# From step 12 on, the causal mask is copied into the scores' bank instead of multiplied in, and the queries' rotation stands earlier in half of the steps

## The chip, the cores and the metric

The kernel runs on one core of a Trainium2 chip. The metric is the device time of one execution in microseconds. The kernel before takes 309.91 us (median of 3 runs, 309.84 to 309.98). Five engines work side by side, each through its own queue in a fixed order: TensorE (PE: matrix products and turns; its weight loads are listed as PEld), VectorE (DVE), ScalarE (ACT), GpSimd (POOL) and SyncE (SP, which issues the DMAs). They wait for each other by counters (semaphores).

## The reference

A block of a decoder layer on x (16 sequences of 64 tokens, 256 wide) with a context of 64 tokens per sequence: gated attention, then a gated feed-forward.

```python
def attention(x, ctx, wq, wk, wv, wo, wk_ctx, wv_ctx, q_norm_w, k_norm_w):
    q = rms_norm(x @ wq, per head of 128, q_norm_w)              # 16 heads
    k = rms_norm(x @ wk, per head of 128, k_norm_w)              # 4 key heads
    v = x @ wv
    k_ctx = rms_norm(ctx @ wk_ctx, per head, k_norm_w); v_ctx = ctx @ wv_ctx
    q = q * cos + rotate_half(q) * sin                           # also k, not k_ctx
    scores = q @ concat(k_ctx, k) * scale + mask                 # 64 x 128 keys for a sequence and head
    # mask: 0 for the context's keys, causal (-inf above the diagonal) for the own keys
    return softmax(scores) @ concat(v_ctx, v) @ wo

x = x + tanh(g_xattn) * attention(layernorm(x), ctx, ...)
gate = silu((h @ fp8(gate_w)) * gate_scale); up = (h @ fp8(up_w)) * up_scale   # h = layernorm(x)
x = x + tanh(g_ffn) * ((gate * up) @ fp8(down_w)) * down_scale
```

## The kernel before

**Tiles and steps.** The 1024 tokens are 8 tiles of 128 (two sequences each). A tile takes four steps, one for each key head and the four query heads that use it. Steps are numbered k = 0 to 31; m = k // 4 is the tile and j = k % 4 the place in it, so "j 0" is a tile's first step and "j 3" its last. In the same four steps the keys and values of the next tile are made and the feed-forward of the tile before is worked off in pieces. Each engine's queue is the same function `one_step` written out for every k, and the order of lines in it is the order of its queue: nothing is scheduled by a program.

**One step on PE.** (1) It turns `q_rot`, the rotated queries of this step (L432), (2) projects the queries of the next step into bank `ps_q` (L409, L414), (3) applies the output projection to the attention of the step before (`ot_hi` by L453, the low part `ot_lo` by L462), (4) turns what is due in this place (`xn` in j 0 and j 2, `k_sin`, the own keys, in j 3), (5) makes the scores in bank `ps_s`, (6) turns the probabilities `probs` of the step before, (7) takes a piece of the feed-forward (`ps_ff`, L561; in j 1 and j 2 behind the next part), (8) projects a part of keys or values and (9) multiplies the turned probabilities `pt` by the values (L752).

**The scores' bank.** `ps_s` holds 128 rows (two sequences of 64 queries) by four heads of 128 keys. Two bf16 matmuls put the mask where own keys stand (L699); they open the bank, and 16 f32 matmuls of keys and queries (L704) add on top. These 18 use tiles of 64 columns of PE's array (in the rows of the profile: 128\*64), everything else on PE uses 128\*128.

**The softmax's loop over the engines.** DVE takes the rows' maximum from `ps_s` (L1245) and makes `exp_bias` (L1248). ACT takes the exponential in four parts (`probs`, L950). DVE inverts the sums (`row_inv`, L1304), POOL multiplies them in (L1470). In the next step PE turns `probs`, and ACT copies them out as `pt` (L926).

**The queries' way.** PE's projection into `ps_q` releases `q_made`. ACT squares it and sums (L785, four ACTIVATEs with their sums; `q_squared`), DVE multiplies `ps_q` by cosine and sine (`q_rot` L1105, `q_sin` L1109), POOL adds the two (L1426), and PE turns the sum as the first thing of the next step. Before the change DVE waits for `q_squared`, so the rotation is behind ACT's squares. From the sum of squares DVE makes `ssq_eps` (L1274) and POOL the scale `q_scale` (L1377), which goes into `exp_bias`.

**Other names that stand around the change.** On DVE: `ot_lo` (L1159); the gate and `fuse` of the feed-forward (L1121 `const`, L1137 `fuse`), whose result the feed-forward on PE waits for one piece later; `xt_lo`<-`ps_transposed` (L1229, j 0), the low part of the tokens turned in this step; `k_var` (L1236, j 2), from which POOL makes `k_inv` for the own keys; `xn` (L1185, j 3), the normalized tokens that PE turns in the next step. On POOL `fuse_lo` (L1388) and `probs` (L1470). On ACT `ot_hi` (L862), `qt` (L869, the copy of the turned queries), `fuse_hi` (L794), and up to step 15 one `o_hi` of 128x1024 a step (L773), while the output weights are still being split.

Of the kernel before, what the change touches and what calls it, by code (L numbers as in the profile page):

```python
# [12 lines left out]
P = 128  # L13
# [81 lines left out]
def build(nc, x, ctx_in, wq, wk, wv, wo, wk_ctx, wv_ctx,  # L95
# [5 lines left out]
    with ExitStack() as stack:  # L101
        def sb(name, shape, dt=f32):
            return stack.enter_context(nc.sbuf_tensor(name, shape, dt))
# [4 lines left out]
        def sem(name):  # L108
            return stack.enter_context(nc.semaphore(name))
# [294 lines left out]
        def _(pe):  # L404
# [225 lines left out]
            def one_step(u, k):  # L630
# [60 lines left out]
                if is_step(u, k):  # L691
# [4 lines left out]
                    scores = four(ps_s)  # L696
                    for r in range(2):
                        rows = slice(r * LEN, (r + 1) * LEN)
                        nc.tensor.matmul(scores[rows, :, rows], ident_bf[:, rows],  # L699
                                         mask[:, :].unsqueeze(1).broadcast_to([P, HPG, LEN]),  # L700
                                         start=True, stop=False, skip_group_check=True)
# [65 lines left out]
        def _(act):  # L767
# [47 lines left out]
            def square_queries(u, k):  # L815
# [3 lines left out]
                if is_step(u, k + 1):  # L819
                    act.wait_ge(q_made, step(u, k + 1) + 1)  # L820
                    if is_step(u, k):
# [25 lines left out]
            def one_step(u, k):  # L847
# [152 lines left out]
        def _(dve):  # L1000
# [95 lines left out]
            def rotate_queries(u, k):  # L1096
# [67 lines left out]
            def one_step(u, k):  # L1164
# [11 lines left out]


                if j == 3 and is_tile(u, m + 2):
                    dve.wait_ge(ln_inv_ready, tile(u, m + 2) + 1)
# [36 lines left out]

                if at_step(u, k) != 0:
                    rotate_queries(u, k)
# [6 lines left out]


                if j == 0 and is_tile(u, m + 1) and tile(u, m + 1) >= TOKENS_SPLIT_FROM:
                    dve.wait_ge(xt_hi_ready, tokens_split(tile(u, m + 1)))
                    nc.vector.tensor_tensor(xt[1][:, nxt, 0:KC, :].rearrange("p c n -> p (c n)"), ps_t[:, 0:HID],  # L1229
                                            as_f32(xt[0][:, nxt, 0:KC, :].rearrange("p c n -> p (c n)")), ALU.subtract)\  # L1230
                        .then_inc(xt_lo_ready, 1)

                if j == 2 and is_tile(u, m + 1):
                    dve.wait_ge(ks_squared, tile(u, m + 1) + 1)
                    dve.wait_ge(kc_inv_ready, tile(u, m + 1) + 1)
                    nc.vector.tensor_scalar(k_var[:, :], k_ssq[:, :], 1.0 / DIM, RMS_EPS, ALU.mult, ALU.add)\  # L1236
                        .then_inc(ks_var_ready, 1)

# [12 lines left out]
                if at_step(u, k) == 0:  # L1251
                    rotate_queries(u, k)


                if j == 2 and is_tile(u, m + 2):
# [119 lines left out]
        def _(pool):  # L1375
# [3 lines left out]
            def fuse_rest(u, slot):  # L1379
# [22 lines left out]
            def one_step(u, k):  # L1402
# [9 lines left out]


                fuse_rest(u, FF_LATE.get(k - 1))

# [7 lines left out]

                if is_step(u, k + 1):
                    pool.wait_ge(q_sin_ready, step(u, k + 1) + 1)
                    nc.gpsimd.tensor_tensor(q_rot[:, :, :], q_rot[:, :, :], q_sin[:, :, :], ALU.add)\  # L1426
                        .then_inc(q_rot_ready, 1)

# [43 lines left out]


            def first_roots():

# [89 lines left out]
```

## Time and profile before

| what | us |
|---|---|
| median of 3 runs | 309.91 (309.84 to 309.98) |
| the profiled execution: its own time | 310.24 |
| its span, first to last instruction | 308.0 |
| around the span | 2.24 |
| PE busy | 294.0 (95%) |
| ACT busy | 232.1 (75%) |
| DVE busy | 231.3 (75%) |
| POOL busy | 183.4 (60%) |
| granted TensorE clock | 1.000 |

The span is one execution as the hardware profiler took it. Busy is the time in which an engine ran an instruction; PE's ends of matmuls are modelled, so where it matters the distance from one start to the next is read instead. A row of the timeline gives start and duration in us and, in brackets, the idle time ahead of it with what ended that. A row of the lines or of a source gives count, busy time and mean. The granted clock is 1.000 throughout, the upper of its two levels (2.4 GHz), so that no part of the time hangs on it.

### The profile page before, as it was taken

To read this page: it belongs to the slowest core of one execution; us is meant where nothing else is said; L and a number is where in the kernel's file an instruction comes from. 1 tells how busy PE (TensorE), PEld (TensorE's weight loads), DVE (VectorE), ACT (ScalarE), POOL (GpSimd) and SP (SyncE) were. 2 spreads that over 40 slices of the span, in tenths; PEclk is the share of its full clock that TensorE was granted. 3 is DMA by queue.
4 is the path that set the end of the run, shared out by engine and by line. 5 is a ranking of instruction groups with operands and counts; after the bars stand their busy time and mean duration, and the time that the engine had idled before them with its cause. 6 is when DMAs were issued, how large, how long until landed. Compare 5 with 4: busy or idle time off the path is not lost.

```text
span 308.0 us, 6587 instructions
## 1 busy us (share of the span) xinstructions
PE 294.0 (95%) x2243; PEld 235.3 (76%) x2243; DVE 231.3 (75%) x482; ACT 232.1 (75%) x893; POOL 183.4 (60%) x178
## 2 busy tenths in 40 slices
PE   7898989998999999999999999999999999988876
PEld 3345666666877888888888888888888888877865
DVE  1768997899899987879864876768765975686553
ACT  2586889977879788998887778787887678776632
POOL 1446685677648695567755685457746684556230
PEclk9999999999999999999999999999999999999999
DMA  6999000000000010001000010000000000000001
GB/s 198 388 390 397 24 17 2 0 1 10 11 3 1 2 34 2 0 2 36 2 0 2 0 37 0 3 0 20 2 1 2 0 19 2 2 0 19 0 0 36
DMA packets 6720, 12.84 MB, mean 42 GB/s; under 512 B 800, under 2 KB 4256, under 8 KB 6688
## 3 DMA queue, kind: packets, MB, share of 16 engines
q1 hardware_dynamic: 6688, 12.43, 11.3%
q8 instruction: 18, 0.29, 0.4%
q14 instruction: 14, 0.11, 0.1%
HBM read 11.38 MB, written 1.05 MB: 40 GB/s over the span
## 4 chain that ended last, share of the span: by engine, by line
PE 28%; ACT 28%; DVE 26%; issue 8%; POOL 5%; DMA 2%; SPq 1%; DVEq 0%; POOLq 0%
ACT probs L950 11%; ACT squares L785 6%; PE ps_y L446 4%; DVE row_max L1245 4%; DVE exp_bias L1248 4%; DVE q_sin L1109 4%; DVE q_rot L1105 3%; ACT qt L869 3%; PE ps_attn L752 3%; PE ps_scores L704 3%; ACT const L842 2%; PE ps_transposed L432 2%; PE ps_kv L420 2%; DMA q_raw<-in_wq_dram 2%; PE ps_probs L432 2%
## 5 line engine op out<-in xcount | busy, mean ns | idle before, releaser
L950 ACT ACTIVATE probs<-ps_scores,exp_bias,q_scale 128x128 f32<-128x128 f32 x128 | 56.9, 455 | 23.7 <-DVE exp_bias L1248 23.6
L1426 POOL TENSOR_TENSOR q_rot<-q_rot,q_sin 128x512 f32<-128x512 f32 x31 | 40.0, 1292 | 18.4 <-DVE q_sin L1109 18.1
L1470 POOL TENSOR_TENSOR probs<-probs,row_inv 128x512 f32<-128x512 f32 x32 | 36.2, 1133 | 17.9 <-DVE row_inv L1304 17.8
L1377 POOL TENSOR_TENSOR q_scale<-ssq_eps,minus_half 128x4 f32<-128x4 f32 x32 | 39.8, 1244 | 10.6 <-DVE ssq_eps L1274 9.6
L1388 POOL TENSOR_TENSOR fuse_lo<-fuse,fuse_hi 128x256 fp32r<-128x256 f32 x21 | 15.4, 733 | 41.3 <-ACT fuse_hi L794 41.3
L785 ACT ACTIVATE squares<-ps_q 128x128 bf16<-128x128 f32 x128 | 34.1, 292 | 5.8 <-PE ps_q L414 4.1
L752 PE MATMUL ps_attn<-pt,values 128*128 128x256 f32 x128 | 33.4, 383 | 0.0
L704 PE MATMUL ps_scores<-kt,qt 128*64 128x128 f32 x512 | 33.3, 273 | 0.0
L926 ACT ACTIVATE pt<-ps_probs 128x512 f32<-128x512 f32 x32 | 19.2, 600 | 13.3 <-PE ps_probs L432 13.3
L704 PEld LDWEIGHTS ps_scores<-kt,qt 128*64 128x64 f32 x512 | 28.9, 137 | 0.0
L1105 DVE TENSOR_TENSOR q_rot<-ps_q,rope 128x512 f32<-128x512 f32 x31 | 21.3, 686 | 9.7 <-ACT squares L785 9.7
L785 ACT ACTIVATION_READ_ACCUMULATOR squares<-ps_q 128x1 f32 x128 | 27.8, 222 | 0.0
L752 PEld LDWEIGHTS ps_attn<-pt,values 128*128 128x128 f32 x128 | 23.1, 190 | 5.4 <-issue 2.9
L950 ACT ACTIVATION_READ_ACCUMULATOR probs<-ps_scores,exp_bias,q_scale 128x1 f32 x128 | 25.7, 201 | 0.0
L1377 POOL TENSOR_TENSOR k_inv<-k_var,minus_half 128x4 f32<-128x4 f32 x16 | 16.6, 1038 | 12.0 <-DVE k_var L1340 5.3
L1304 DVE RECIPROCAL row_inv<-row_sum 128x4 f32<-128x4 f32 x32 | 5.6, 174 | 24.1 <-ACT probs L950 24.1
L1245 DVE TENSOR_REDUCE row_max<-ps_scores 128x4 f32<-128x512 f32 x32 | 21.8, 681 | 1.5 <-PE ps_scores L704 1.5
L453 PE MATMUL ps_y<-o_hi,ot_hi 128*128 128x256 f32 x88 | 22.0, 285 | 0.2 <-ACT ot_hi L862 0.2
L432 PE MATMUL ps_probs<-const,probs 128*128 128x128 f32 x128 | 21.0, 286 | 1.1 <-POOL probs L1470 1.1
L453 PE MATMUL ps_y<-o_lo,ot_hi 128*128 128x256 f32 x88 | 21.4, 278 | 0.0
L409 PE MATMUL ps_q<-q_hi,xt_hi 128*128 128x512 f32 x48 | 21.0, 436 | 0.4 <-issue 0.4
L785 ACT ACTIVATE squares<-ps_kv 128x128 bf16<-128x128 f32 x60 | 15.9, 290 | 7.2 <-DVE k_sin L1206 4.5
(195 smaller groups left out, 839.2 us busy)
## 6 DMA issues: line engine op xcount, KB each, us to landing
q_raw<-in_wq_dram SPq DMA_DIRECT2D x4, 512.0 KB, 8.3
o_raw<-in_wo_dram SPq DMA_DIRECT2D x4, 512.0 KB, 12.3
ctx_t<-in_ctx_dram SPq DMA_DIRECT2D x8, 128.0 KB, 2.7
out_dram<-x_sb SPq DMA_DIRECT2D x8, 128.0 KB, 1.7
stage<-in_gate_w_dram SPq DMA_DIRECT2D x2, 384.0 KB, 10.1
stage<-in_up_w_dram SPq DMA_DIRECT2D x2, 384.0 KB, 11.1
x_sb<-in_x_dram SPq DMA_DIRECT2D x1, 768.0 KB, 13.1
stage<-in_down_w_dram SPq DMA_DIRECT2D x2, 384.0 KB, 13.1
```

The source lines that it names most:

```text
L409: nc.tensor.matmul(dst, lhs(0, i), rhs(b, i), start=(i == 0 and b == 0), stop=False)
L432: last = nc.tensor.matmul(dst[:, i * P:(i + 1) * P], src, ident, start=True, stop=True, is_transpose=True)
L453: nc.tensor.matmul(ps_y[:, 0:HID], ot_hi[:, h, :], w_o[b][:, g0, h, :], start=(g0 == 0 and h == 0 and b == 0), stop=False)
L704: last = nc.tensor.matmul(scores[r * LEN:(r + 1) * LEN, h, :], qt[:, r, h, :], kt[:, par, j, 2 * r:2 * r + 2, :], start=False, stop=(h == ...
L752: last = nc.tensor.matmul(ps_o[:, r * 256:(r + 1) * 256], values[:, p0, r, g0 * DIM:(g0 + 1) * DIM], pt[:, :].rearrange("p (h r l) -> p r ...
L785: last = nc.scalar.activation(squares[:, h, :], src[:, h * DIM:(h + 1) * DIM], ACT.Square, accum_out=dst[:, h:h + 1])
L950: last = nc.scalar.activation(probs[:, i, :], ps_s[:, i * P:(i + 1) * P], ACT.Exp, bias=exp_bias[:, i:i + 1], scale=q_scale[:, k % 2, i:i ...
L1105: nc.vector.tensor_tensor(q_rot[:, :, :], four(ps_q), over_heads(rope[:, 0, :]), ALU.mult)\
L1245: nc.vector.tensor_reduce(row_max[:, :], four(ps_s), AX.X, ALU.max).then_inc(max_ready, 1)
L1377: return nc.gpsimd.tensor_tensor(dst, src, minus_half[:, 0:src.shape[1]], ALU.pow)
L1426: nc.gpsimd.tensor_tensor(q_rot[:, :, :], q_rot[:, :, :], q_sin[:, :, :], ALU.add)\
L1470: nc.gpsimd.tensor_tensor(probs[:, :, :], probs[:, :, :], row_inv[:, :].unsqueeze(2).broadcast_to([P, 4, P]), ALU.mult).then_inc(probs_rea ...
```

## The change

**The mask (k from 12 to 31, 20 steps).** The two mask matmuls are left out. GpSimd fills an f32 tile `mask_all` of 128x128 once, in the prologue (one memset and two small copies; const in SBUF as source). In each of these steps an engine copies it, repeated over four heads, into `ps_s` (128x512): VectorE in j 0, 1 and 3, behind `ot_lo` (15 steps), ScalarE in j 2, behind `qt` (5 steps). The copy waits for `exp_ready` of the step before (the exponential has read the bank), the scores wait for `mask_set` of the copy, and add onto what it wrote.

**The rotation (`ROTATE_FIRST`: k = 12, 15, 16, 19, 20, 23, 24, 27, 28, 31; the last has no next queries).** DVE's `q_rot` and `q_sin` stand directly behind the mask copy, ahead of `xn`, the gate and `fuse`, and wait for `q_made` instead of `q_squared`; POOL's addition stands ahead of `fuse_lo`. ACT's squares in turn wait for `q_sin_ready`. PE's next projection into `ps_q` waits for `q_squared` too, and so does `ssq_eps` (both in all steps).

**Two operations moved in all steps.** DVE's `xt_lo` of the tokens (j 0) and `k_var` (j 2) stand behind `row_max` and `exp_bias` instead of ahead of them.

```diff
+ROTATE_FIRST = tuple(k for k in range(12, STEPS) if k % GROUPS in (3, 0))
+MASK_COPIED_FROM = 12
...
 # PE
                     if is_step(u, k):
                         pe.wait_ge(q_sin_ready, step(u, k) + 1)
+                        pe.wait_ge(q_squared, step(u, k) + 1)
...
-                    for r in range(2):
+                    if step(u, k) >= MASK_COPIED_FROM:
+                        pe.wait_ge(mask_set, step(u, k) - MASK_COPIED_FROM + 1)
+                    for r in range(2 if step(u, k) < MASK_COPIED_FROM else 0):
...
 # ACT: square_queries
                 if is_step(u, k + 1):
-                    act.wait_ge(q_made, step(u, k + 1) + 1)
+                    if step(u, k) in ROTATE_FIRST:
+                        act.wait_ge(q_sin_ready, step(u, k + 1) + 1)
+                    else:
+                        act.wait_ge(q_made, step(u, k + 1) + 1)
...
 # ACT: behind qt
+                if is_step(u, k) and step(u, k) >= MASK_COPIED_FROM and j == 2:
+                    act.wait_ge(exp_ready, step(u, k))
+                    act.wait_ge(mask_filled, 1)
+                    nc.scalar.activation(four(ps_s), mask_all[:, :].unsqueeze(1).broadcast_to([P, HPG, P]), ACT.Copy)\
+                        .then_inc(mask_set, 1)
...
 # DVE
+            def set_mask(s):
+                if s == MASK_COPIED_FROM:
+                    dve.wait_ge(mask_filled, 1)
+                dve.wait_ge(exp_ready, s)
+                nc.vector.tensor_copy(four(ps_s), mask_all[:, :].unsqueeze(1).broadcast_to([P, HPG, P])).then_inc(mask_set, 1)
...
-                    dve.wait_ge(q_squared, step(u, k + 1) + 1)
+                    if step(u, k) in ROTATE_FIRST:
+                        dve.wait_ge(q_made, step(u, k + 1) + 1)
+                    else:
+                        dve.wait_ge(q_squared, step(u, k + 1) + 1)
...
+                if is_step(u, k) and step(u, k) >= MASK_COPIED_FROM and j != 2:
+                    set_mask(step(u, k))
+                if at_step(u, k) in ROTATE_FIRST:
+                    rotate_queries(u, k)
                 if j == 3 and is_tile(u, m + 2):
                     dve.wait_ge(ln_inv_ready, tile(u, m + 2) + 1)
...
                 if is_step(u, k + 1):
                     if is_step(u, k):
                         dve.wait_ge(q_scale_ready, step(u, k) + 1)
+                    dve.wait_ge(q_squared, step(u, k + 1) + 1)
                     nc.vector.tensor_scalar(ssq_eps[:, :], ssq[:, :], DIM * RMS_EPS, None, ALU.add)\
                         .then_inc(ssq_moved, 1)
...
 # POOL
+                if at_step(u, k) in ROTATE_FIRST:
+                    add_rotated(u, k)
                 fuse_rest(u, FF_LATE.get(k - 1))
...
+                if at_step(u, k) not in ROTATE_FIRST:
+                    add_rotated(u, k)
```

DVE's queue in step 12 (j 0), the kernel before; `const` is the gate's product, `ps_ff` a bank of the feed-forward:

```order
193 L1159 TENSOR_TENSOR ot_lo<-ps_attn,ot_hi 128x2x4x64 [waits ot_hi_ready]
194 L1121 SCALAR_TENSOR_TENSOR const<-const,ps_ff 128x256 [waits tanh_ready]
195 L1137 SCALAR_TENSOR_TENSOR fuse<-const,fuse_scale,ps_ff 128x128 [waits fuse_lo_ready,gated_ready]
197 L1105 TENSOR_TENSOR q_rot<-ps_q,rope 128x512 [waits q_turned,q_squared]
198 L1109 TENSOR_TENSOR q_sin<-ps_q,rope 128x512 [waits q_rot_ready]
199 L1229 TENSOR_TENSOR xt_lo<-ps_transposed,xt_hi 128x256 [waits xt_hi_ready]
200 L1245 TENSOR_REDUCE row_max<-ps_scores 128x4 [waits scores_made]
201 L1248 SCALAR_TENSOR_TENSOR exp_bias<-row_max,q_scale 128x4 [waits q_scale_ready,max_ready]
202 L1274 TENSOR_SCALAR ssq_eps<-ssq 128x4 [waits q_scale_ready]
```

The same step of the changed kernel (its line numbers are its own):

```order
193 L1189 TENSOR_TENSOR ot_lo<-ps_attn,ot_hi 128x2x4x64 [waits ot_hi_ready]
194 L1099 COPY ps_scores<-mask_all 128x512 [waits exp_ready,mask_filled]
195 L1135 TENSOR_TENSOR q_rot<-ps_q,rope 128x512 [waits q_turned,q_made]
196 L1139 TENSOR_TENSOR q_sin<-ps_q,rope 128x512 [waits q_rot_ready]
197 L1151 SCALAR_TENSOR_TENSOR const<-const,ps_ff 128x256 [waits tanh_ready]
198 L1167 SCALAR_TENSOR_TENSOR fuse<-const,fuse_scale,ps_ff 128x128 [waits fuse_lo_ready,gated_ready]
200 L1270 TENSOR_REDUCE row_max<-ps_scores 128x4 [waits scores_made]
201 L1273 SCALAR_TENSOR_TENSOR exp_bias<-row_max,q_scale 128x4 [waits q_scale_ready,max_ready]
202 L1282 TENSOR_TENSOR xt_lo<-ps_transposed,xt_hi 128x256 [waits xt_hi_ready]
203 L1312 TENSOR_SCALAR ssq_eps<-ssq 128x4 [waits q_squared,q_scale_ready]
```

Three operations of 128x512 (the copy, `q_rot`, `q_sin`) now stand between `ot_lo` and the gate, none between `fuse` and `row_max`. In j 3 it is the same with `xn` behind `q_sin`.

PE's queue in step 15 (j 3), the kernel before, around the mask:

```order
569 L432 MATMUL ps_transposed<-const,k_sin 128x128 [waits ks_ready,qt_ready]
570 L432 MATMUL ps_transposed<-const,k_sin 128x128 x3
571 L699 MATMUL ps_scores<-mask,ident_bf 64x4x64 x2
572 L704 MATMUL ps_scores<-kt,qt 64x128 x8
573 L432 MATMUL ps_probs<-const,probs 128x128 [waits probs_ready]
```

The same place of the changed kernel (each of the rows of the scores counts pairs, one matmul for each sequence):

```order
565 L439 MATMUL ps_transposed<-const,k_sin 128x128 [waits ks_ready,qt_ready]
566 L439 MATMUL ps_transposed<-const,k_sin 128x128 x3
567 L714 MATMUL ps_scores<-kt,qt 64x128 [waits mask_set]
568 L714 MATMUL ps_scores<-kt,qt 64x128 x7
569 L439 MATMUL ps_probs<-const,probs 128x128 [waits probs_ready]
```

The two mask matmuls are gone and the first of the scores waits for the copy.

## Rows read from the trace of the kernel before

**Rows 1.** The page: busy time of the engines, and the chain that ended last
```profile
PE 294.0 (95%) x2243; PEld 235.3 (76%) x2243; DVE 231.3 (75%) x482; ACT 232.1 (75%) x893; POOL 183.4 (60%) x178
PE 28%; ACT 28%; DVE 26%; issue 8%; POOL 5%; DMA 2%; SPq 1%; DVEq 0%; POOLq 0%
```
**Rows 2.** Windows, tiles 4 and 5: window, length, busy, PEclk
```profile
157.30:192.14 34.84, 34.69 (x290) 30.06 (x289) 24.57 (x55) 27.49 (x113) 21.65 (x23) 1.00 0.03 9
192.14:226.60 34.46, 34.46 (x289) 30.06 (x288) 24.57 (x55) 27.11 (x112) 21.54 (x22) 1.00 0.02 6
```
**Rows 3.** Timeline of PE around the mask, step 23: start, us, engine, line
```profile
221.26 0.60 PE L432 MATMUL ps_transposed<-const,k_sin 128*128 128x128 f32 x4
221.79 0.30 PE L699 MATMUL ps_scores<-mask,ident_bf 128*64 128x256 bf16 x2
221.92 1.04 PE L704 MATMUL ps_scores<-kt,qt 128*64 128x128 f32 x16
222.89 0.66 PE L432 MATMUL ps_probs<-const,probs 128*128 128x128 f32 x4
223.39 0.39 PE L561 MATMUL ps_ff<-x2t_hi,w_ff 128*128 128x128 f16 x4
```
**Rows 4.** Timeline of PE: step 20's start, and its feed-forward piece
```profile
192.14 0.60 PE L432 MATMUL ps_transposed<-const,q_rot 128*128 128x128 f32 x4
192.49 0.47 PE L409 MATMUL ps_q<-q_hi,xt_hi 128*128 128x512 f32 x1
...
197.35 0.61 PE L561 MATMUL ps_ff<-x2t_hi,w_ff 128*128 128x128 f16 x8
```
**Rows 5.** Timeline of DVE, step 20
```profile
194.13 0.68 DVE L1159 TENSOR_TENSOR ot_lo<-ps_attn,ot_hi 128x512 fp32r<-128x512 f32 x1
...
195.17 0.61 DVE L1137 SCALAR_TENSOR_TENSOR fuse<-const,fuse_scale,ps_ff 128x128 f32<-128x128 f32 x2
196.65 0.69 DVE L1105 TENSOR_TENSOR q_rot<-ps_q,rope 128x512 f32<-128x512 f32 x1 [0.88 <-ACT squares L785]
...
198.19 0.68 DVE L1245 TENSOR_REDUCE row_max<-ps_scores 128x4 f32<-128x512 f32 x1
198.90 0.42 DVE L1248 SCALAR_TENSOR_TENSOR exp_bias<-row_max,q_scale 128x4 f32<-128x4 f32 x1
```
**Rows 6.** Timeline of POOL, steps 20 and 23
```profile
198.02 1.29 POOL L1426 TENSOR_TENSOR q_rot<-q_rot,q_sin 128x512 f32<-128x512 f32 x1 [0.29 <-DVE q_sin L1109]
...
219.76 1.04 POOL L1470 TENSOR_TENSOR probs<-probs,row_inv 128x512 f32<-128x512 f32 x1
```
**Rows 7.** Timeline of DVE, steps 21 to 23
```profile
203.28 0.17 DVE L1194 TENSOR_SCALAR k_var<-k_ssq 128x4 f32<-128x4 f32 x1 [0.83 <-ACT squares L785]
...
219.86 1.09 DVE L1185 TENSOR_SCALAR xn<-x_sb,ln_mean,ln_inv 128x256 f32<-128x256 f32 x1
...
221.32 0.61 DVE L1137 SCALAR_TENSOR_TENSOR fuse<-const,fuse_scale,ps_ff 128x128 f32<-128x128 f32 x2
```
**Rows 8.** Timeline of ACT: steps 12, 20 and 22
```profile
128.62 1.06 ACT L773 ACTIVATE o_hi<-o_raw 128x1024 fp32r<-128x1024 f32 x1
...
197.55 0.60 ACT L926 ACTIVATE pt<-ps_probs 128x512 f32<-128x512 f32 x1 [0.35 <-PE ps_probs L432]
...
211.73 0.28 ACT L785 ACTIVATE squares<-ps_q 128x128 bf16<-128x128 f32 x1 [0.75 <-PE ps_q L414]
```
**Rows 9.** Timeline of DVE, step 2
```profile
37.44 0.17 DVE L1236 TENSOR_SCALAR k_var<-k_ssq 128x4 f32<-128x4 f32 x1
```
**Rows 10.** Timeline of PE, step 3
```profile
44.91 0.33 PE L432 MATMUL ps_probs<-const,probs 128*128 128x128 f32 x1 [0.84 <-POOL probs L1470]
```
**Rows 11.** Timeline of DVE, last tile (steps 28 and 31)
```profile
267.19 0.73 DVE L1248 SCALAR_TENSOR_TENSOR exp_bias<-row_max,q_scale 128x4 f32<-128x4 f32 x1
...
285.06 0.69 DVE L1159 TENSOR_TENSOR ot_lo<-ps_attn,ot_hi 128x512 fp32r<-128x512 f32 x1 [0.84 <-ACT ot_hi L862]
```
**Rows 12.** Timeline of PE, step 31
```profile
285.56 0.30 PE L699 MATMUL ps_scores<-mask,ident_bf 128*64 128x256 bf16 x2 [0.74 <-ACT qt L869]
```

More of the change, by code:

```diff
@@ L114, in build @@
         ident_bf = sb("ident_bf", [P, P], bf16)
+        mask_all = sb("mask_all", [P, P])
         ident = const[:, C_ID:C_ID + P]
@@ L211, in build @@
         half_set = sem("half_set")
+        mask_cleared, mask_filled, mask_set = sem("mask_cleared"), sem("mask_filled"), sem("mask_set")
         tables_ready = sem("tables_ready")
@@ L1215, in one_step @@
                                             k_inv[:, :].unsqueeze(2).broadcast_to([P, HPG, DIM]), ALU.mult).then_inc(kc_ready, 1)
-                if at_step(u, k) != 0:
+                if at_step(u, k) not in ROTATE_FIRST and at_step(u, k) != 0:
                     rotate_queries(u, k)
@@ L1224, in one_step @@
                                             ALU.subtract).then_inc(x2_lo_ready, 1)
[L1227 to L1237, printed above, removed]
                 if at_step(u, k) in SHORT_OF_VECTOR:
@@ L1252, in one_step @@
                     rotate_queries(u, k)
+                if j == 0 and is_tile(u, m + 1) and tile(u, m + 1) >= TOKENS_SPLIT_FROM:
+                    dve.wait_ge(xt_hi_ready, tokens_split(tile(u, m + 1)))
+                    nc.vector.tensor_tensor(xt[1][:, nxt, 0:KC, :].rearrange("p c n -> p (c n)"), ps_t[:, 0:HID],
+                                            as_f32(xt[0][:, nxt, 0:KC, :].rearrange("p c n -> p (c n)")), ALU.subtract)\
+                        .then_inc(xt_lo_ready, 1)
+                if j == 2 and is_tile(u, m + 1):
+                    dve.wait_ge(ks_squared, tile(u, m + 1) + 1)
+                    dve.wait_ge(kc_inv_ready, tile(u, m + 1) + 1)
+                    nc.vector.tensor_scalar(k_var[:, :], k_ssq[:, :], 1.0 / DIM, RMS_EPS, ALU.mult, ALU.add)\
+                        .then_inc(ks_var_ready, 1)
                 if j == 2 and is_tile(u, m + 2):
@@ L1393, in fuse_rest, with add_rotated @@
                         .then_inc(result_ready, 1)
+            def add_rotated(u, k):
+                if is_step(u, k + 1):
+                    pool.wait_ge(q_sin_ready, step(u, k + 1) + 1)
+                    nc.gpsimd.tensor_tensor(q_rot[:, :, :], q_rot[:, :, :], q_sin[:, :, :], ALU.add)\
+                        .then_inc(q_rot_ready, 1)
             def quantize_store(i):
@@ L1421, in one_step @@
                         .then_inc(ks_added, 1)
[L1424 to L1427, printed above, removed]
+                if at_step(u, k) not in ROTATE_FIRST:
+                    add_rotated(u, k)
                 if ROUND_AT.get(k - 1, 0) >= WIDE:
@@ L1471, in one_step, with fill_mask @@
                                             row_inv[:, :].unsqueeze(2).broadcast_to([P, 4, P]), ALU.mult).then_inc(probs_ready, 1)
+            def fill_mask():
+                nc.gpsimd.memset(mask_all[:, :], 0.0).then_inc(mask_cleared, 1)
+                pool.wait_ge(mask_cleared, 1)
+                pool.wait_ge(const_in, 16)
+                for r in range(2):
+                    rows = slice(r * LEN, (r + 1) * LEN)
+                    last = nc.gpsimd.tensor_copy(mask_all[rows, rows], const[rows, C_MASK:C_MASK + LEN])
+                last.then_inc(mask_filled, 1)
+                pool.wait_ge(mask_filled, 1)
             def first_roots():
@@ L1494, in _ @@
             first_roots()
+            fill_mask()
             run_steps(pool, one_step)
```

## The prediction

> **What bounds the kernel now.** I read the page first: PE is busy for 95% of the span and no other engine for more than 76%, yet the chain that ended last spends as much time on ACT (28%) and DVE (26%) as on PE (28%) [rows 1]. The reader is to see two bounds close together. The windows settle which holds: in tile 5 PE is busy for 34.46 of 34.46 us, in tile 4 for 34.69 of 34.84, with the granted clock at 1.00 [rows 2]. Tile 4 is 0.38 longer: one late `ot_lo` in its first step. So PE sets the pace in steps 12 to 27, and the loop exponential, `ot_hi`, `qt`, squares, rotation, `row_max`, `exp_bias` runs beside it with almost no room: whatever PE saves is worth something only if that loop becomes as much shorter. Last I read the timelines of DVE, POOL and ACT for what the loop waits on. The profiled execution took 310.24, its span 308.0, so 2.24 lie around it; the median of the runs is 309.91, that is 0.33 below the profiled one. I sum against the span, add 2.24, take 0.33 off.
>
> **The mask on PE.** In step 23 it is 0.53 us from the start of the four turns to the mask, 0.13 from there to the scores (221.79 to 221.92), 0.97 to the turn of `probs` [rows 3]. The same four turns ahead of a full-sized matmul take 0.35 (192.14 to 192.49) [rows 4]. So entering the 64-column tiles costs 0.18, and this cost belongs to the first 64-column matmul, mask or scores. With the mask gone the 0.13 goes, but the scores' first weight load, now hidden beside the mask, is exposed: I put that at about 0.05, the 0.18 of an entry being about half load. 0.13 - 0.05 = 0.08 a step is my value. From below: 0.03, if the load and the added wait for `mask_set` show almost whole; from above: 0.08 + 0.15 = 0.23, if the entry cost goes along with the mask. PE binds in 16 of the 20 steps (12 to 27): 16 x 0.08 = 1.3 (0.5 to 3.7).
> The Trainium skill ("TensorEngine Tiling (Array Packing)", Key Properties) says that a change of the tiling mode drains TensorE. By it the entry cost stays as long as the scores keep their 64-column tiles, which speaks for 0.08 and against 0.23; the trace agrees with a cost at the change (0.18).
>
> **The copy.** No row before shows an f32 copy from SBUF into PSUM. Nearest rows: DVE's 128x512 operations with one PSUM operand, 0.68 each, the next one 0.60 later [rows 5]. From below 0.35, if it ran at the pace of an operation that touches SBUF alone; from above 0.7. I take 0.60. On ACT likewise 0.60, that of its own 128x512 copy out of PSUM [rows 8].
> The Trainium skill ("VectorE: DVE Perf Modes", Why PSUM operands drop a tier) says an operation with a PSUM operand has no use of both SBUF ports and runs f32 at the plain rate. By it the copy costs 0.60 and doesn't stand in POOL's way; at 0.35 the sum would be the same, since the copy is off PE's path.
> Cover, place by place. In j 2 ACT is idle for 0.75 ahead of its squares [rows 8]: the copy fits. In j 1 DVE is idle for 0.83 ahead of `k_var` [rows 7]: fits. In j 0 and j 3 it has no such gap ahead of the gate, but the 0.88 of idle time ahead of `q_rot` in j 0 [rows 5], which the rotation gives up by moving ahead, pays for it: DVE's total work in the step becomes 0.60 more, its idle time 0.6 less. In time for PE: in step 20 the copy would run from 194.73 to 195.4; the scores start 0.97 + 0.50 ahead of the feed-forward piece (221.92, 222.89, 223.39), that is at 195.88 [rows 3, 4]; no wait.
>
> **The rotation first.** Between `ot_lo` and the gate stand 3 x 0.60 = 1.8 us more. `fuse` in step 20 ends at 195.78 and PE wants it at 197.35, slack 1.57 [rows 4, 5]; in step 23 it ends at 221.93 against 223.39, slack 1.46 [rows 3, 7]. So by itself the insert is late by 0.2 to 0.35. What pays is the start: `row_max` in step 20 begins at 198.19, though the scores were made at about 196.9 (195.88 + 0.97), because `q_rot`, `q_sin` and `xt_lo` stood ahead of it [rows 3, 5]. Now it begins at 196.95 or behind `fuse`. `exp_bias` moreover lasts 0.42 there and 0.73 in step 28, for 128x4, and ends in step 20 as POOL's addition does (198.90 + 0.42, 198.02 + 1.29) [rows 5, 6, 11]; now that addition is over earlier, and `exp_bias` should take about the 0.17 of `k_var`, of the same shape [rows 7]. I put exponential, `row_inv`, `probs` and next `ot_lo` at 0.8 to 0.9 earlier in j 0 and j 3, 0.5 in j 2 (`k_var` behind `exp_bias`, POOL out of the way), 0.3 in j 1. With 0.8 earlier, `fuse` is in time by 0.5. Hence in steady state nothing is lost, and what PE waited for in these steps goes: 0.38 in tile 4 [rows 2] and a few waits of less than 0.1 in tiles 4 to 6, 0.6 in all.
> ACT's squares wait for the rotation, about 1.3 later at the earliest, but the rotation is itself ahead by 1.3, so they start about where they did (195.5); PE's next projection comes 6 us behind, and the added waits for `q_squared` cost nothing.
>
> **Start of the regime.** In step 12 no exponential was early, and DVE's insert pushes `fuse` and ACT's squares by 0.3 to 1.2; behind them ACT still runs an `o_hi` of 1.06 [rows 8] ahead of the exponential. I take +0.5 over steps 12 and 13 (0 to 1.0).
> **`k_var` early.** In step 2 it moves from 37.44 behind `row_max` and `exp_bias`, each up to 0.7, to about 38.8. POOL's addition of 1.29 covers all but about 0.3 of that, then its `k_inv` is late, and behind it `probs`, for which PE waits 0.84 in step 3 [rows 6, 9, 10]: +0.2 (0 to 0.4).
> **The last tile.** From step 28 PE waits for the loop, not the loop for PE. `exp_bias` of step 28 lasts 0.73 beside POOL's addition [rows 11]; rotation ahead frees some 1.0. But in steps 29 and 31 the copy on DVE stands behind `ot_lo`: in step 31 `ot_lo` starts at 285.06, the copy would end at 286.3, and the mask matmuls went at 285.56 [rows 11, 12]; 0.7 of the gain goes back there, and less in step 29. Net -0.75 (-1.2 to +0.3).
>
> **Sum.** -1.3 - 0.6 + 0.5 + 0.2 - 0.75 = -1.95: span 306.05, execution 308.3, median 307.95, so I say 307.9. Its own range, with the bounds of the terms combined and not all at one end: 306.6 to 309.2.
>
> **Rivals.**
> (A) The entry cost goes with the mask: 0.23 a step, 16 x 0.15 = 2.4 more, 305.5. For it: the mask is bf16 and the scores f32, so part of the 0.18 may be the mask's own. Against it: leaving the 64-column tiles for the turn of `probs`, all f32, shows a gap of the same kind, and the loop on ACT and DVE may not give so much. 0.10.
> (B) No net change: the loop stays as long as it was, since DVE has the copy's 0.60 more in three of four steps; PE then waits for what it saved. The 1.3 of the mask is lost; the 0.6 and some 0.5 of the tail stay, against +0.7 of the start and `k_var`: -0.4, 309.5. For it: the chain has equal shares of ACT, DVE and PE. Against: the 1.2 by which `row_max` stands late in step 20. 0.18.
> (C) Slower: DVE is too full in j 3. `xn` moves behind `q_sin`, just when POOL starts its addition of 1.29. `xn` touches SBUF alone; beside POOL's `probs` (219.76 + 1.04) it lasts 1.09, to that one's end [rows 6, 7]. Caught behind the addition, it and the gate behind it end 0.9 late, PE waits for `fuse` in steps 15, 19, 23 and 27. That is 4 x 0.9 = 3.6 against -1.95: +1.65, 311.5. It decides as soon as `xn` starts after POOL's addition instead of the 0.08 before `q_sin`'s end, at which DVE's next operation usually starts; that is what speaks against it. 0.13.
>
> **How the numbers follow.** Forecast 0.59, A 0.10, B 0.18, C 0.13. What a measurement here can tell from no change is 0.2%, 0.62 us (309.29 to 310.53). Faster: forecast all but 0.01, A, and 0.03 of B: 0.71. Same: 0.01 of the forecast, 0.14 of B, 0.01 of C: 0.16. Slower: 0.12 of C, 0.01 of B: 0.13. Range: A's centre at its lower end, B with its spread at the upper, 305.4 to 310.0, which leaves C and little of A and B out.
>
> **What would show it.** Right: the distance from the last turn to the scores falls by about 0.08 and the 0.18 of the entry stays; tiles 4 to 6 take 34.1 instead of 34.46 with PE busy throughout; copies of 0.68 on DVE and 0.60 on ACT; `exp_bias` at about 0.17 in j 0 and j 3; `xn` at 0.3 ahead of POOL's addition. Wrong: idle time on PE ahead of the scores with `mask_set` as its releaser, ahead of `ps_ff` with `fuse`, or `ot_hi` in j 2 later; then the time is B's or C's. A distance of 0.35 from turns to scores would be A.

## The result and the profile after

The changed kernel takes 308.08 us (median of 4 runs, 307.98 to 308.20) against 309.95 (309.84 to 310.36) on the same chip: ratio 0.9937, interval 0.9924 to 0.9949. It is 1.87 us faster; 1.95 and a time of 307.9 were forecast. The span of the profiled execution is 306.2 instead of 308.0, the granted clock 1.000 as before. In two of the experiments below single runs took 1.5 to 1.8 us longer than the others, with a granted clock of 0.994 to 0.995 (one of eleven of mask alone, two of five of copy twice); they raise those two ratios and hardly the medians.

Not the whole gain lies in the span. The time around it is 308.09 - 306.2 = 1.88 instead of the 2.24 before. In every run of the eight kernels in which ScalarE copies a mask it lies between 1.77 and 1.99, in every run of the four without such a copy (before, order alone, rotation alone, all on VectorE) between 2.07 and 2.26. So some 0.3 of the 1.87 lies outside the span and goes with ScalarE's copies; the traces begin and end with the span, and the cause stays open.

The page after, busy time and chain [rows 1]:

```profile
PE 292.1 (95%) x2203; PEld 233.4 (76%) x2203; DVE 230.2 (75%) x497; ACT 234.6 (77%) x898; POOL 183.1 (60%) x181
PE 70%; DVE 13%; ACT 6%; issue 4%; POOL 3%; DMA 2%; SPq 1%; DVEq 0%; POOLq 0%
```

The chain went from equal shares of PE, ACT and DVE to 70% on PE: nothing but PE's own work now stands in most of it. The windows of tiles 4 and 5 [rows 2] say the same:

```profile
157.74:191.69 33.95, 33.95 (x281) 29.64 (x280) 24.22 (x59) 27.73 (x111) 21.56 (x23) 1.00 0.03 9
191.69:225.65 33.96, 33.96 (x282) 29.65 (x281) 24.23 (x59) 27.73 (x111) 21.59 (x23) 1.00 0.02 6
```

Tile 5 takes 33.96 instead of 34.46, PE without a gap in both tiles. The timeline of PE in step 23 [rows 3] shows what the mask was worth:

```profile
220.39 0.60 PE L439 MATMUL ps_transposed<-const,k_sin 128*128 128x128 f32 x4
220.92 1.09 PE L714 MATMUL ps_scores<-kt,qt 128*64 128x128 f32 x16
221.94 0.66 PE L439 MATMUL ps_probs<-const,probs 128*128 128x128 f32 x4
```

The turns' 0.53 is unchanged and now stands ahead of the scores; the scores take 1.02 instead of 0.97, and the mask's 0.13 is gone. The loads of the scores begin at 220.91, after a wait, not beside the matmuls before:

```profile
220.91 0.85 PEld L714 LDWEIGHTS ps_scores<-kt,qt 128*64 128x64 f32 x16 [0.17 <-issue]
```

DVE in step 20 [rows 5], and POOL's addition [rows 6] with `fuse_lo` behind it:

```profile
192.57 0.68 DVE L1189 TENSOR_TENSOR ot_lo<-ps_attn,ot_hi 128x512 fp32r<-128x512 f32 x1
193.17 0.68 DVE L1099 COPY ps_scores<-mask_all 128x512 f32<-128x512 f32 x1
193.77 0.67 DVE L1135 TENSOR_TENSOR q_rot<-ps_q,rope 128x512 f32<-128x512 f32 x1
194.37 0.67 DVE L1139 TENSOR_TENSOR q_sin<-ps_q,rope 128x512 f32<-128x512 f32 x1
194.96 0.40 DVE L1151 SCALAR_TENSOR_TENSOR const<-const,ps_ff 128x256 f32<-128x256 f32 x1
195.40 0.61 DVE L1167 SCALAR_TENSOR_TENSOR fuse<-const,fuse_scale,ps_ff 128x128 f32<-128x128 f32 x2
196.36 0.69 DVE L1270 TENSOR_REDUCE row_max<-ps_scores 128x4 f32<-128x512 f32 x1 [0.35 <-PE ps_scores L714]
197.08 0.26 DVE L1273 SCALAR_TENSOR_TENSOR exp_bias<-row_max,q_scale 128x4 f32<-128x4 f32 x1
```

```profile
195.12 1.27 POOL L1437 TENSOR_TENSOR q_rot<-q_rot,q_sin 128x512 f32<-128x512 f32 x1 [2.75 <-DVE q_sin L1139]
196.60 0.73 POOL L1426 TENSOR_TENSOR fuse_lo<-fuse,fuse_hi 128x256 fp32r<-128x256 f32 x1 [0.20 <-ACT fuse_hi L804]
```

DVE now waits for the scores (0.35) ahead of `row_max`, where before the scores waited for DVE; `row_max` starts 4.67 after the step's start (191.69) instead of 6.05. `exp_bias` takes 0.26, no longer held to the end of POOL's addition, which is over at 196.39; it ends at 197.34 as POOL's `fuse_lo` does (196.60 + 0.73), which is why it is 0.26 and not the 0.17 that were forecast. In step 23 `xn` [rows 7] starts 0.17 ahead of POOL's addition and takes 0.40 instead of 1.09:

```profile
220.41 0.40 DVE L1222 TENSOR_SCALAR xn<-x_sb,ln_mean,ln_inv 128x256 f32<-128x256 f32 x1
220.58 1.37 POOL L1437 TENSOR_TENSOR q_rot<-q_rot,q_sin 128x512 f32<-128x512 f32 x1 [0.60 <-DVE q_sin L1139]
```

The 1.8 us by which the span is shorter, from the starts of the steps in both traces: up to step 12 +0.25 (0.07 in step 3, 0.22 in step 9, less jitter), steps 12 to 14 +0.5 beside the masks, 16 masks x 0.079 = -1.26, waits that vanished in steps 15 to 27 -1.0, the last tile -0.34. The 16 masks are a way of counting: in steps 12 to 14 PE waits for the loop, and both masks (below), which keeps the matmuls there, is no later at step 15 (+0.55 against +0.54).

The loss in step 12 and the one in the last tile have rows of their own. PE waits for `fuse` in step 12, and for DVE's copy in steps 28, 29 and 31 [rows 12]:

```profile
128.44 0.61 PE L568 MATMUL ps_ff<-x2t_hi,w_ff 128*128 128x128 f16 x8 [0.20 <-DVE fuse L1167]
...
261.87 1.09 PE L714 MATMUL ps_scores<-kt,qt 128*64 128x128 f32 x16 [0.27 <-DVE ps_scores L1099]
...
269.11 1.09 PE L714 MATMUL ps_scores<-kt,qt 128*64 128x128 f32 x16 [0.51 <-DVE ps_scores L1099]
...
284.02 1.09 PE L714 MATMUL ps_scores<-kt,qt 128*64 128x128 f32 x16 [1.87 <-DVE ps_scores L1099]
```

### The profile page after: what moved, and what is told of

Same layout as the page of the kernel before. It is cut to its first block, busy times and chain, and to the rows that moved or that the text cites. A ratio compares the mean times of both kernels' runs of the same rounds, so it can differ in the third digit from the quotient of the medians.

```text
span 306.2 us, 6572 instructions
## 1 busy us (share of the span) xinstructions
PE 292.1 (95%) x2203; PEld 233.4 (76%) x2203; DVE 230.2 (75%) x497; ACT 234.6 (77%) x898; POOL 183.1 (60%) x181
## 4 chain that ended last, share of the span: by engine, by line
PE 70%; DVE 13%; ACT 6%; issue 4%; POOL 3%; DMA 2%; SPq 1%; DVEq 0%; POOLq 0%
PE ps_scores L714 8%; PE ps_attn L762 7%; PE ps_q L416 6%; PE ps_transposed L439 6%; PE ps_kv L416 6%; PE ps_y L460 6%; PE ps_ff L568 5%; PE ps_probs L439 5%; PE ps_y L453 4%; PE ps_q L421 3%; PE ps_ff L590 3%; PE ps_y L469 3%; PE ps_kv L421 3%; PE ps_kv L427 2%; DMA q_raw<-in_wq_dram 2%
## 5 line engine op out<-in xcount | busy, mean ns | idle before, releaser
L1415 POOL TENSOR_TENSOR q_scale<-ssq_eps,minus_half 128x4 f32<-128x4 f32 x32 | 36.8, 1150 | 12.5 <-DVE ssq_eps L1312 11.5
L714 PE MATMUL ps_scores<-kt,qt 128*64 128x128 f32 x512 | 34.4, 276 | 2.6 <-DVE ps_scores L1099 2.6
L714 PEld LDWEIGHTS ps_scores<-kt,qt 128*64 128x64 f32 x512 | 28.0, 137 | 6.4 <-ACT qt L882 3.0
L970 ACT ACTIVATION_READ_ACCUMULATOR probs<-ps_scores,exp_bias,q_scale 128x1 f32 x128 | 26.5, 207 | 0.0
L1189 DVE TENSOR_TENSOR ot_lo<-ps_attn,ot_hi 128x512 fp32r<-128x512 f32 x22 | 15.1, 688 | 12.4 <-ACT ot_hi L875 12.4
```

The lines of the kernel that those rows point to most:

```text
L714: last = nc.tensor.matmul(scores[r * LEN:(r + 1) * LEN, h, :], qt[:, r, h, :], kt[:, par, j, 2 * r:2 * r + 2, :], start=False, stop=(h == ...
L970: last = nc.scalar.activation(probs[:, i, :], ps_s[:, i * P:(i + 1) * P], ACT.Exp, bias=exp_bias[:, i:i + 1], scale=q_scale[:, k % 2, i:i ...
L1415: return nc.gpsimd.tensor_tensor(dst, src, minus_half[:, 0:src.shape[1]], ALU.pow)
```

## The experiments

The table has for every kernel the median, and how far it is ahead (-) of or behind (+) the kernel before at the start of PE's turn of `q_rot` in a step, and at PE's last matmul; worked out from the start times of both traces, each set to zero at step 0. All rows are set against the same trace of the kernel before, of an execution that took 310.24, some 0.3 more than the median of that kernel; so each row may show up to 0.3 too much gain, but differences between rows are free of that.

| kernel | median us | step 4 | 12 | 16 | 20 | 24 | 28 | end |
|---|---|---|---|---|---|---|---|---|
| changed | 308.08 | +0.05 | +0.25 | +0.45 | -0.43 | -0.94 | -1.45 | -1.79 |
| order alone | 309.84 | +0.05 | +0.27 | +0.46 | +0.21 | +0.04 | -0.13 | -0.30 |
| rotation alone (with the order) | 308.24 | +0.05 | +0.27 | +0.19 | -0.35 | -0.51 | -0.68 | -1.92 |
| mask alone (with the order) | 309.65 | +0.07 | +0.30 | +0.19 | -0.12 | -0.55 | -0.99 | -0.18 |
| both masks | 309.32 | +0.06 | +0.25 | +0.55 | +0.02 | -0.15 | -0.32 | -0.51 |
| last tile on PE | 307.19 | +0.05 | +0.26 | +0.47 | -0.42 | -0.92 | -1.44 | -2.70 |
| behind from 12 | 308.01 | -0.04 | +0.08 | +0.28 | -0.61 | -1.11 | -1.63 | -1.98 |
| start later | 306.63 | -0.02 | +0.10 | 0.00 | -0.89 | -1.40 | -1.91 | -3.16 |
| few waits | 306.48 | -0.02 | -0.06 | -0.15 | -1.04 | -1.54 | -2.06 | -3.35 |
| copy twice | 314.01 | +0.05 | +0.23 | +1.57 | +1.60 | +1.97 | +2.16 | +3.99 |
| all on VectorE | 310.49 | +0.05 | +0.26 | +1.09 | +0.68 | +0.65 | +0.62 | +0.30 |

**Order alone.**

```diff
-ROTATE_FIRST = tuple(k for k in range(12, STEPS) if k % GROUPS in (3, 0))
+ROTATE_FIRST = ()
-MASK_COPIED = tuple(range(12, STEPS))
+MASK_COPIED = ()
```

(`MASK_COPIED` is a list of steps in place of the changed kernel's first step; all kernels below use it.)

> Only the order on DVE and the added waits for q_squared: xt_lo (j 0) and k_var (j 2) behind row_max and exp_bias in all steps; mask matmuls as before, no rotation first. Theory (the gain is made of the mask's 0.08 a step on PE and of waits that the rotation takes away; this part only costs, early): PE late by 0.07 in step 3 and 0.22 in step 9 as in the trace of the changed kernel, nothing gained from step 12 on: 309.95 + 0.3 = 310.2 us. Rival (the loop is shortened by this order, since row_max comes 0.33 sooner in j 0): tiles 3 to 6 lose their small waits, tile period 34.3 instead of 34.46, 309.4 us.

309.84, ratio 0.9993 (0.9984 to 1.0002): between the two. The early loss of 0.27 is there, and step 14 adds 0.19, but from step 16 on it is won back: tile 4 takes 34.58 instead of 34.84, tiles 5 and 6 take 34.30, as the rival said. In the windows, tile 5:

```profile
192.42:226.72 34.30, 34.30 (x289) 30.00 (x288) 24.17 (x55) 27.24 (x112) 21.54 (x22) 1.00 0.02 6
```

So the small waits of tiles 5 and 6 (34.46 - 34.30 = 0.16) go with the place of `xt_lo` and `k_var` alone. The traces tell which of the two it is. DVE in step 22 (j 2), before and with the order alone:

```profile
215.23 0.80 DVE L1236 TENSOR_SCALAR k_var<-k_ssq 128x4 f32<-128x4 f32 x1
215.95 0.68 DVE L1245 TENSOR_REDUCE row_max<-ps_scores 128x4 f32<-128x512 f32 x1
```

```profile
215.14 0.68 DVE L1271 TENSOR_REDUCE row_max<-ps_scores 128x4 f32<-128x512 f32 x1
215.86 0.16 DVE L1274 SCALAR_TENSOR_TENSOR exp_bias<-row_max,q_scale 128x4 f32<-128x4 f32 x1
215.94 0.17 DVE L1290 TENSOR_SCALAR k_var<-k_ssq 128x4 f32<-128x4 f32 x1
```

`k_var` no longer stands 0.80 ahead of `row_max`: from the start of `q_rot` to the end of `exp_bias` it is 2.78 instead of 3.50. In j 0 the move of `xt_lo` brings `row_max` forward, but `exp_bias` then lasts 0.75 instead of 0.42, to the end of POOL's addition as before: from `q_rot` to its end it is 2.66 instead of 2.68. So the gain is that of `k_var` in j 2, not the rival's earlier `row_max` in j 0.

**Rotation alone.** `MASK_COPIED = ()` and no `mask_all`, rotation and order as changed.

> The changed kernel with the mask matmuls kept in all steps and no copy, no mask_all: rotation first and the order alone. Theory: PE has no wait in tiles 3 to 6, but 0.079 a step more: tile period 33.96 + 0.32 = 34.28; the last tile has no wait for a copy (0.27, 0.51 and 1.87 in the changed kernel), so that it ends up to 1 us sooner than there. In all 308.1 + 1.3 - 0.8 = 308.6 us. Rival (the time comes from the mask alone, the rotation gives nothing): 309.9 to 310.2 us, tile period 34.46.

308.24, ratio 0.9945 (0.9933 to 0.9958). The theory holds in kind (tile 34.30, the last tile -1.24 against -0.34), and the time is 0.4 less than it said. Nearly the whole gain of the change is here, without the mask. Beside order alone tiles 5 and 6 are no shorter; the rotation gains in steps 14 to 19 (0.56: from +0.21 to -0.35 at step 20) and in the last tile (1.24 against 0.17).

**Mask alone.** `ROTATE_FIRST = ()`, copies as changed.

> The changed kernel without rotation first: the mask copied from step 12 on, q_rot and q_sin in their old place behind ACT's squares. Theory (PE and the loop over ACT and DVE are about equally long, so PE's 0.079 a step counts only when the loop gets shorter too): PE waits for ot_lo, kt or fuse what it saved, tile period 34.3 to 34.5, and the last tile waits for the copy: 309.7 to 310.6 us. Rival (PE alone binds, the copy fits into DVE's idle time of 0.5 to 0.9 a step): tile period 34.46 - 0.32 = 34.14, 309.0 us.

309.65, ratio 0.9996 (0.9985 to 1.0007), just under the theory's 309.7. The 0.34 by which the median is under the 309.99 of its kernel before is no more than the 0.3 around the span. But its reason was wrong in steady state: the tile takes 34.03, even under the rival's 34.14.

```profile
191.98:226.01 34.03, 34.03 (x281) 29.66 (x280) 25.99 (x58) 27.77 (x113) 21.49 (x22) 1.00 0.02 6
```

Of the four pairs' 0.32 a tile PE keeps 0.27 beside order alone (34.30 to 34.03), so most of the copy fits into DVE's and ACT's idle time. What makes the time near that of before is the last tile, which loses 0.81 (-0.99 to -0.18): the scores wait for the copy 1.57 in step 29 and 1.91 in step 31.

```profile
270.62 1.09 PE L715 MATMUL ps_scores<-kt,qt 128*64 128x128 f32 x16 [1.57 <-DVE ps_scores L1100]
...
285.57 1.09 PE L715 MATMUL ps_scores<-kt,qt 128*64 128x128 f32 x16 [1.91 <-DVE ps_scores L1100]
```

**Both masks.**

```diff
-                    for r in range(0 if copied else 2):
+                    for r in range(2):
```

> The changed kernel with copy and mask matmuls both (the matmuls open the bank again, so the copy's values are written over). Theory: PE binds in steps 12 to 27, the pair costs 0.134 and hides the 0.055 of the first weight load: +0.079 a step, +1.3 us over 16 steps, nothing in the last tile: 309.3 us; tile period 34.28. Rival (DVE and ACT bind after the change, PE's time is hidden): 308.1 us.

309.32, ratio 0.9979 (0.9970 to 0.9988): the theory to 0.02 us. By the traces the 1.28 between the two kernels is 1.12 in steps 15 to 27, 0.01 in steps 12 to 14 and 0.15 in the last tile. Against the changed kernel the tile takes 34.30 instead of 33.96, and the turns, mask and scores of step 23 are again 0.53, 0.13 and 0.97:

```profile
221.13 0.60 PE L439 MATMUL ps_transposed<-const,k_sin 128*128 128x128 f32 x4
221.66 0.30 PE L710 MATMUL ps_scores<-mask,ident_bf 128*64 128x256 bf16 x2
221.79 1.04 PE L715 MATMUL ps_scores<-kt,qt 128*64 128x128 f32 x16
222.76 0.66 PE L439 MATMUL ps_probs<-const,probs 128*128 128x128 f32 x4
```

So the pair is worth 0.079 a step and PE is what binds; the copy on DVE and ACT costs PE nothing in tiles 4 to 6 (34.30 with it, 34.30 without it in rotation alone).

**Last tile on PE.** `MASK_COPIED = tuple(range(12, STEPS - 4))`.

> The changed kernel, but the last tile's masks (steps 28 to 31) are made by PE's matmuls again; copies in steps 12 to 27 only. Theory: from step 28 the changed kernel's PE waits for DVE's copy (0.27, 0.51, 1.87), and the kernel with rotation alone runs the last tile 0.9 us shorter (from step 28 to the end -1.24 against -0.34 relative to before); so steps 12 to 27 as in the changed kernel and that last tile: 308.08 - 0.9 = 307.2 us. Rival (the copies in the last tile are beside the chain, which ends with the exponential and the feed-forward): 308.1 us.

307.19, ratio 0.9911 (0.9898 to 0.9925): the theory. In step 31 PE now waits for `qt` only, as before the change:

```profile
282.77 0.30 PE L710 MATMUL ps_scores<-mask,ident_bf 128*64 128x256 bf16 x2 [0.74 <-ACT qt L883]
```

**Behind from 12.** `xt_lo` and `k_var` in their old place in steps 0 to 11.

> The changed kernel with xt_lo (j 0) and k_var (j 2) in their old place, ahead of row_max, in steps 0 to 11, and behind exp_bias only from step 12. Theory: the 0.07 in step 3 and the 0.22 in step 9 go: 308.08 - 0.29 = 307.8 us. Rival (the loss is taken up by later waits, so it does not arrive at the end): 308.1 us.

308.01, ratio 0.9935 (0.9922 to 0.9947). The trace is 0.19 ahead at the end: step 3 wins its 0.08, but step 9 only 0.07 of its 0.22. The medians of the two kernels, from two chips, differ by 0.07 only, too little to tell. What remains in step 9 (0.14) was not the order.

**Start later.** Both of these, and copies from step 13, rotation first from step 15.

```diff
-ROTATE_FIRST = tuple(k for k in range(12, STEPS) if k % GROUPS in (3, 0))
+ROTATE_FIRST = tuple(k for k in range(13, STEPS) if k % GROUPS in (3, 0))
-MASK_COPIED = tuple(range(12, STEPS))
+MASK_COPIED = tuple(range(13, STEPS - 4))
+BEHIND_FROM = 12
```

> All three together: order behind exp_bias from step 12, copies in steps 13 to 27, rotation first from step 15 (not in 12), last tile's masks on PE. Theory: against the changed kernel -0.9 (last tile), -0.29 (order) and -0.35 (step 12: PE's wait for fuse of 0.37 against the 0.08 of one mask pair): 308.08 - 1.5 = 306.6 us. Rival (without the early rotation of step 12 the waits of steps 14 to 16, 0.6 us, stay longer): 307.0 us.

306.63, ratio 0.9894 (0.9879 to 0.9909): the theory again, 1.45 us under the changed kernel (by the traces 1.37). The later start was not run by itself; its share is read from the trace. Against last tile on PE, the way from PE's turn of `probs` to the feed-forward piece in step 12 is 0.37 shorter, the mask pair 0.079 longer.

**Few waits.**

```diff
-                        pe.wait_ge(q_squared, step(u, k) + 1)
+                        if step(u, k) - 1 in ROTATE_FIRST:
+                            pe.wait_ge(q_squared, step(u, k) + 1)
```

and the same for `ssq_eps` on DVE.

> The kernel with the later start, but PE's and ssq_eps's added wait for q_squared only where the rotation stood first (elsewhere q_sin_ready already implies it). Theory (in step 9 PE starts 0.26 us after q_lo is ready instead of 0.10 before the change, since one more wait stands in its queue): -0.15 in step 9 and nothing elsewhere, 306.5 us, step 9 back at 8.72 to 8.73 between turn and projection's first weights. Rival (the 0.15 is not from the wait): 306.63 us and step 9 unchanged.

306.48, ratio 0.9880 (0.9866 to 0.9893). From the turn to the projection in step 9 it is 1.15 with the added wait (start later, first) and 1.00 without (few waits, second); DVE's `q_lo`, for which PE waits there, ends 0.89 and 0.90 behind the turn:

```profile
95.09 0.60 PE L440 MATMUL ps_transposed<-const,q_rot 128*128 128x128 f32 x4
96.24 0.47 PE L417 MATMUL ps_q<-q_hi,xt_hi 128*128 128x512 f32 x1 [0.55 <-DVE q_lo L1038]
```

```profile
95.03 0.60 PE L440 MATMUL ps_transposed<-const,q_rot 128*128 128x128 f32 x4
96.03 0.47 PE L417 MATMUL ps_q<-q_hi,xt_hi 128*128 128x512 f32 x1 [0.40 <-issue]
```

ACT's squares, for which the added wait stands, had ended at 90.4, long before, and nevertheless the wait cost 0.15, in the one step in which PE stands at this place for something else. In steps 10 to 30 the distance is 0.36 in both kernels. This is the fastest kernel of the study, 3.67 us under its before.

**Copy twice.** Each copy of VectorE made a second time, behind the first.

> The changed kernel with each of VectorE's mask copies made twice (the second waits for the first), 15 times 0.6 to 0.7 us more on DVE. Theory (in tiles 4 to 6 DVE is close to the bound: fuse is ready some 0.7 us ahead of PE's need in j 0 and j 3, and DVE idles only 0.3 ahead of row_max): half of it shows, +0.1 to 0.3 a step in j 0 and j 3, tile period 34.2 to 34.5, and the last tile +1.5: 310.5 us. Rival (DVE has room): tile period 33.96, only the last tile longer, 309.3 us. Rival (DVE is the bound): +0.6 a step, 315 us.

314.01, ratio 1.0146 (1.0124 to 1.0168), far over the 310.5 of the theory and under the second rival's 315: tiles 4 to 6 take 34.87, 34.83 and 34.66. Of the 5.8 by which it is behind the changed kernel in the traces, 1.1 arise before step 16, 2.5 in tiles 4 to 6 and 2.2 in the last tile. In step 20 PE's feed-forward piece starts 1.12 behind the turn of `probs` instead of 0.50:

```profile
199.29 0.61 PE L569 MATMUL ps_ff<-x2t_hi,w_ff 128*128 128x128 f16 x8 [0.46 <-DVE fuse L1171]
```

The doubled copy puts 0.7 ahead of the gate, but then `exp_bias` too is late enough to meet POOL's `fuse_lo`:

```profile
199.78 0.71 DVE L1277 SCALAR_TENSOR_TENSOR exp_bias<-row_max,q_scale 128x4 f32<-128x4 f32 x1
```

```profile
199.73 0.73 POOL L1430 TENSOR_TENSOR fuse_lo<-fuse,fuse_hi 128x256 fp32r<-128x256 f32 x1 [0.21 <-ACT fuse_hi L806]
```

Both end together (200.49 and 200.46), 0.45 more than the 0.26 of the changed kernel. In j 3 the same happens, and `ot_lo` of the next j 0 starts 1.36 behind the step's start instead of 0.88. So in j 0 the gate is late by 0.72 + 0.48 = 1.20 and PE by 0.62: the slack behind one copy is some 0.6 us, and what is late beyond it costs more than itself.

**All on VectorE.** The mask of j 2 is copied by DVE behind `xn`, ScalarE copies none.

> The changed kernel with the mask of j 2 copied by VectorE behind ot_lo too, ScalarE copies none. Theory (DVE has no idle time ahead of row_max in j 2 but 0.28 ahead of x2t_lo, ACT had 0.26 left behind its copy): row_max of j 2 comes 0.3 to 0.5 later, ot_lo of j 3 has 0.78 idle ahead of it and takes most of that up: tile period 33.96 to 34.2, 308.1 to 308.9 us, likeliest 308.4. Rival (DVE is the bound, as two copies a step showed it close to it): +0.6 a tile and +2.4 us, 310.5 us.

310.49, ratio 1.0012 (1.0003 to 1.0021): the rival's 310.5, but with 0.48 a tile (34.43) instead of its 0.6, and by a chain that neither had named. PE waits in each j 2 for ACT's squares of the own keys, which wait for DVE's `k_sin`:

```profile
215.37 0.47 PE L416 MATMUL ps_kv<-kv_hi,xt_hi 128*128 128x512 f32 x1 [0.25 <-ACT squares L796]
```

From the turn of `probs` to this row it is 0.91 (214.46 to 215.37) instead of 0.42. In the changed kernel the same place shows no wait; there DVE has no copy ahead of `k_sin`. So ScalarE's five copies are worth 2.4 us beside VectorE's by the medians; 2.1 of it by the traces (+0.30 against -1.79), and 0.3 lies around the span (2.2 against 1.9).

## Why the prediction was right, and where not

**The mask on PE.** The price was right, and the entry cost with it: 0.53, 0.079 and 1.02 were 0.53, 0.08 and 0.97 + 0.05. Both masks shows it on the whole time, +1.24. But PE binds from step 15 on, in 13 of the 16 steps that were counted: 13 x 0.079 = 1.03 would have been the term (1.12 by both masks). Rival A (0.23 a step) falls: the 0.18 stays when no bf16 mask is there. That a change of the tiling mode drains TensorE (the Trainium skill, "TensorEngine Tiling (Array Packing)", Key Properties) agrees with these numbers.

**The copy.** Right: 0.682 on DVE, the next operation 0.60 later, 0.61 on ACT, and it did not wait for POOL. In tiles 4 to 6 the cover was as read. In the last tile it was not: see below.

**The waits that vanish.** 0.6 forecast, about 1.0 measured. Tile 4 lost its 0.38 and in addition the 0.18 that tiles 5 and 6 lost; I counted the 0.38 as if it held both. The cause was put at the rotation, and in tiles 5 and 6 this was wrong: order alone has the same 34.30 as rotation alone. `row_max` of j 2 was late because of `k_var`, held to the end of POOL's addition; its move was enough, and that of `xt_lo` in j 0 gave 0.02. In tile 4 the rotation was needed too (34.30 against 34.58 with the order alone). With the mask copied too, the rotation gives 0.07 a tile more (33.96 against 34.03).

**The rotation's 1.8 us ahead of the gate.** Right that the earlier start pays for it from step 15 on, and by more than was said: counted from the step's start, `exp_bias` ends 1.5 sooner in j 0, 1.2 in j 3, 0.9 in j 2 and 0.4 in j 1, where 0.8 to 0.9, 0.5 and 0.3 were put. ACT's squares start where they did (3.38 against 3.34 in step 20), as forecast. Rival C (`xn` caught behind POOL's addition) falls: `xn` starts 0.17 ahead of it and takes 0.40.

**Start of the regime.** +0.5 forecast, +0.5 measured beside the masks. It needs copy and rotation together: in rotation alone step 12 loses nothing, in mask alone neither.

**`k_var` early and the added waits.** +0.2 was forecast for step 3; measured are 0.07 there and 0.22 in step 9, the latter made of 0.07 by the order and 0.15 by the wait for `q_squared`, which I had put at nothing. The sum was about right, the place was not. The traces show both ways: in step 2 `k_inv` on POOL waits 0.18 for the later `k_var`, and PE waits 0.91 instead of 0.84 for POOL's `probs`. In step 8 `xt_lo` stands ahead of `ssq_eps`, and DVE's `q_lo` behind it ends 0.96 after PE's turn instead of 0.90.

**The last tile.** -0.75 forecast, -0.34 measured. This is the mis-sized term. The rotation frees more than the 1.0 I gave (rotation alone -1.24), and the copies take 0.90 back (last tile on PE against the changed kernel: -1.26 against -0.34). My own parts, 1.0 freed and 0.7 and something given back, did not add up to -0.75 either, but to -0.3 at most.

**As a whole** the time was hit by errors that cancel: 0.4 too little of vanished waits against 0.4 too much in the last tile. Two more cancel outside the steps: I left the 2.24 around the span as it was, where 1.88 was measured, and took off 0.33 for a profiled execution slower than its median, where the changed kernel's is slower by 0.01 only. That the time came within 0.2 of the forecast is therefore in part luck. And it hid what matters most: on top of the rotation the mask gives nothing in the span. The medians have 0.16 (308.24 to 308.08), of which more than all is the time around the span (2.1 to 1.9), and by the traces from step 0 on the kernel with the mask is 0.13 behind (-1.92 against -1.79). The mask gains 1.04 from step 16 to 28 and gives back 0.27 before step 16 and 0.90 in the last tile. Rival B's picture, gain made and spent, holds for the mask by itself (309.65), by another mechanism than DVE's load in steady state.

Not settled: what shortens the time around the span by 0.3, and what the mask is worth in the fastest kernel, which was not run with the mask matmuls in all steps. In the copied steps the scores' matmuls add onto a bank that the mask matmuls of steps 0 to 11 had opened; whether a bank that no matmul has opened yet can be preset so, no run here shows.

## What to carry to other kernels

Work taken from the bounding engine pays only in the stages in which that engine binds. At the pipeline's start and end, where it waits for the loop through the other engines, the same move lengthens the loop; so give such a change a first and a last step of its own, and read each stage's window separately. When several edits come together, run each alone: here the mask's copy was worth almost nothing as placed. With its two ends cut off the kernel is 1.6 us under rotation alone (308.24 to 306.63); by the traces it is 1.24, some 0.2 of it the order's in steps 0 to 11, which leaves about 1.0 for the mask.

## What the runs showed of the hardware

A wait on a semaphore that is long satisfied cost 0.15 us where it stood in PE's queue just ahead of another that was really waited for (step 9), and nothing in steps 10 to 30. A DVE operation of 128x4 in SBUF (`exp_bias`, `k_var`) lasted 0.16 to 0.81 us in steps 12 to 31 by what POOL did: begun while POOL's addition or `fuse_lo` ran, it ended within 0.03 of them, unless its own 0.16 took longer. Beside a POOL operation of 128x4 it was not held (`exp_bias` 0.16 beside `k_inv`), and `xn`, begun 0.17 ahead of POOL's addition, kept 0.40. DVE's operations of 128x512 with a PSUM operand kept 0.65 to 0.70. The first weight load behind a change from 128 to 64 columns began behind 0.17 of idle time on PEld in step 23, with the mask and without, and so did the one behind the change back; without the mask some 0.05 of it shows (1.02 against 0.97).
